# A block of attention: queries, keys and probabilities turned by VectorE blocks and a way through device memory

## The reference

```python
x = x + _L0_xattn_ref(_layernorm(x, axis=-1), ctx_4096, Wq, Wk, Wv, Wo, q_norm_w, k_norm_w)

def _L0_xattn_ref(latents, context, Wq, Wk, Wv, Wo, q_norm_w, k_norm_w):
    kv = jnp.concatenate([context, latents], axis=1)
    q = (latents @ Wq).reshape(bsz, q_len, HEADS, HEAD_DIM).transpose(0, 2, 1, 3)
    k = (kv @ Wk).reshape(bsz, kv_len, KV_HEADS, HEAD_DIM).transpose(0, 2, 1, 3)
    v = (kv @ Wv).reshape(bsz, kv_len, KV_HEADS, HEAD_DIM).transpose(0, 2, 1, 3)
    q = rms_norm(q, q_norm_w)
    k = rms_norm(k, k_norm_w)
    qg = q.reshape(bsz, KV_HEADS, groups, q_len, HEAD_DIM)
    scores = jnp.einsum('bhgqd,bhkd->bhgqk', qg, k) * scale
    probs = jax.nn.softmax(scores.astype(jnp.float32), axis=-1).astype(q.dtype)
    out = jnp.einsum('bhgqk,bhkd->bhgqd', probs, v)
    return out @ Wo
```

## Time and profile before

| | us |
|---|---|
| Median of 3 runs | 1143.39 (1141.55 to 1143.66) |
| Profiled execution | 1142.94 |
| Its span in the trace | 1141.1 |
| TensorE busy, matmuls | 1097.6 |
| VectorE / ScalarE / GpSimd busy | 773.4 / 523.9 / 398.5 |

### The profile page before, as it was taken

One profiled execution on the slowest core, in us unless ns is written; L12 is line 12 of the kernel. 1 busy time (PEld: TensorE's weight loads), 2 busy tenths in 40 slices (PEclk: granted clock), 3 DMA queues, 4 the chain that ended last, 5 costly groups with the idle time before them and its releaser, 6 DMA issues. The chain is left out here.

```text
span 1141.1 us, 18735 instructions
## 1 busy us (share of the span) xinstructions
PE 1097.6 (96%) x6533; PEld 950.9 (83%) x6533; DVE 773.4 (68%) x1496; ACT 523.9 (46%) x1398; POOL 398.5 (35%) x385
## 2 busy tenths in 40 slices
PE   4899999999999999999999999999999999888998
PEld 3789899998989999898989989878877777677877
DVE  7577777777777777777777765764344566889863
ACT  4354544545455454544544444443223445465531
POOL 4443343433334343343434321210002334575521
PEclk7899999999999999999999999999999999999999
DMA  6322323332332323233232120022202244143300
GB/s 221 82 79 71 104 63 98 88 96 69 92 103 64 97 89 96 68 102 106 70 103 84 50 91 1 1 80 89 65 1 56 65 111 111 43 104 77 84 10 37
DMA packets 65376, 89.05 MB, mean 78 GB/s; under 512 B 15544, under 2 KB 35024, under 8 KB 65284
## 3 DMA queue, kind: packets, MB, share of 16 engines
q1 hardware_dynamic: 60788, 70.95, 22.0%
q0 software_dynamic: 4496, 16.91, 4.8%
HBM read 64.64 MB, written 10.74 MB: 66 GB/s over the span
## 5 line engine op out<-in xcount | busy, mean ns | idle before, releaser
L366 PE MATMUL bank<-wqkv,kvT 128*128 128x256 f32 x1536 | 199.9, 286 | 2.1 <-DVE vv L570 2.1
L418 PE MATMUL bank<-wo,aoT 128*128 128x512 f32 x768 | 191.8, 398 | 0.0
L366 PEld LDWEIGHTS bank<-wqkv,kvT 128*128 128x128 f32 x1536 | 187.9, 191 | 3.7 <-DVE vv L570 3.6
L354 PE MATMUL bank<-wqkv,kvT 128*128 128x512 f32 x768 | 189.1, 395 | 1.6 <-DVE qn L585 1.6
L354 PEld LDWEIGHTS bank<-wqkv,kvT 128*128 128x128 f32 x768 | 141.8, 191 | 28.9 <-issue 1.8
L418 PEld LDWEIGHTS bank<-wo,aoT 128*128 128x128 f32 x768 | 139.6, 188 | 27.2
L671 POOL TENSOR_TENSOR rms<-msq,half_neg 128x4 f32<-128x4 f32 x64 | 80.0, 1249 | 202.7 <-DVE msq L581 202.5
L527 ACT ACTIVATE qsq<-bank 128x512 f32<-128x512 f32 x64 | 38.2, 597 | 115.3 <-PE bank L354 115.3
L553 ACT ACTIVATE prob<-bank,nmax 128x128 f32<-128x128 f32 x256 | 90.1, 371 | 2.2 <-DVE nmax L595 2.2
L585 DVE TENSOR_TENSOR qn<-bank,rms 128x512 f32<-128x512 f32 x64 | 44.3, 692 | 61.0 <-POOL rms L671 61.0
L674 POOL TENSOR_TENSOR rms<-msq,half_neg 128x2 f32<-128x2 f32 x64 | 44.8, 699 | 116.5 <-DVE msq L591 116.5
(11 more groups left out here) (176 smaller groups left out, 2131.1 us busy)
## 6 DMA issues: line engine op xcount, KB each, us to landing
wqkv_raw<-in_L_xattn_Wq_dram SPq DMA_DIRECT2D x32, 256.0 KB, 2.6
wo_raw<-in_L_xattn_Wo_dram SPq DMA_DIRECT2D x32, 256.0 KB, 2.8
qS<-qhl SPq DMA_DIRECT2D x32, 256.0 KB, 3.8
wload<-w_gu SPq DMA_DIRECT2D x20, 256.0 KB, 3.2
w_gu<-qch SPq DMA_DIRECT2D x16, 256.0 KB, 2.3
kS<-chl SPq DMA_DIRECT2D x32, 128.0 KB, 3.1
qch<-_L_ffn_down_qweight_dram SPq DMA_DIRECT2D x10, 256.0 KB, 3.6
w_d<-qch SPq DMA_DIRECT2D x10, 256.0 KB, 2.0
```

Source lines behind the costliest of these rows:

```text
L354: mm = pe.matmul(b_q[:, :], kvT[:, l, kt, p, 1:3, :], wqkv[:, par, r, kt, 0:QW], start=(kt == 0 and n == 0), stop=(kt == KT - 1 and n == 2))
L366: mm = pe.matmul(b_kv[:, b * 256:(b + 1) * 256], kvT[:, l, kt, p, 2 * b:2 * b + 2, :], wqkv[:, par, r, kt, QW:QKV], start=(kt == 0 and n = ...
L418: mm = pe.matmul(b_o[:, :], aoT[:, l, h, :, :], wo[:, par, r, h, :], start=(h == 0 and n == 0), stop=(h == G - 1 and n == 2))
```

## The change

The transposes by TensorE go. In place of them VectorE turns blocks of 32 x 32 numbers: it writes the normalized tile into a PSUM bank `b_n` in an order in which every fourth column stands together, and transposes blocks from there to SBUF (`qB`, `kB`, `pB`). SyncE stores the tile to device memory (`q_turn`, `k_turn`, `p_turn`, 256, 128 and 256 KB) and loads it back with whole blocks in their places (`blocks_out`, `blocks_back`). Queries arrive in `qT`; keys in `kT`, where ScalarE scales them in place; probabilities in the LO half of `pT`, from which ScalarE rounds HI, and VectorE subtracts in place at the head of its next step.

Squares are now summed by ScalarE's accumulator, in four and two instructions, so VectorE's two reductions go. Keys and values alternate between two banks. TensorE's scores move to the end of the step, its values product from unit j-2 to j-3 and to the place behind the query projection; exponentials and normalization move to unit j-2; the sum into `acc` (L566) moves from unit j-4 at the head to unit j-3 at the end of VectorE's list. The dequantization pieces stand behind the maxima and ahead of the key normalization. The first three weight tiles of the second part are loaded within the loop, in its steps 62 to 64.

```diff
+            def sp_step0(st):
+                if st.has(1, UNITS):
+                    sp.wait_ge(s_k_out, st.done(1, 16))
+                    wait(sp, s_s, st.done(2))
+                    blocks_back(sp, kT[:, :, :, :], k_turn).then_inc(s_k_back, 16)
+                if st.has(2, UNITS):
+                    sp.wait_ge(s_pB, st.done(2))
+                    wait(sp, s_p_back, st.done(3, 16))
+                    blocks_out(sp, p_turn, pB[:, :, :, :]).then_inc(s_p_out, 16)
+                if st.j >= 1:
+                    weight_load(st.j - 1)
+                sp_stores(sp, st.j)
...
+                for f in WLOAD_AT.get(st.j - EVEN_DONE, ()):
+                    weight_tile(sp, f)
+                if st.has(2, UNITS):
+                    sp.wait_ge(s_p_out, st.done(2, 16))
+                    wait(sp, s_pv, st.done(3))
+                    blocks_back(sp, pT[:, LO, :, :, :].bitcast(F32), p_turn).then_inc(s_p_back, 16)
+                if st.has(0, UNITS):
+                    sp.wait_ge(s_qB, st.done(0))
+                    wait(sp, s_q_back, st.done(1, 16))
+                    blocks_out(sp, q_turn, qB[:, :, :, :]).then_inc(s_q_out, 16)
+                sp_loads(sp, st.j)
+                if st.has(0, UNITS):
+                    sp.wait_ge(s_kB, st.done(0))
+                    wait(sp, s_k_back, st.done(1, 16))
+                    blocks_out(sp, k_turn, kB[:, :, :, :]).then_inc(s_k_out, 16)
+                    sp.wait_ge(s_q_out, st.done(0, 16))
+                    wait(sp, s_s, st.done(1))
+                    blocks_back(sp, qT[:, :, :, :], q_turn).then_inc(s_q_back, 16)
+        def blocks_out(sp, to, frm):
+            return sp.dma_start(to.rearrange("a p r -> (a p r)").rearrange("(p c) -> p c", p=P),
+                                frm.rearrange("p b h t -> p (b h t)"))
+        def blocks_back(sp, to, frm):
+            return sp.dma_start(to.rearrange("p a h t -> p a (h t)"), frm.rearrange("a p r -> p a r"))
...
         def dve_step0(st):
+            if st.has(3, UNITS):
+                dve.wait_ge(s_phi, st.done(3))
+                dve.tensor_tensor(pT[:, LO, :, :, :].rearrange("p h b t -> p (h b t)"),
+                                  pT[:, LO, :, :, :].rearrange("p h b t -> p (h b t)").bitcast(F32),
+                                  pT[:, HI, :, :, :].rearrange("p h b t -> p (h b t)").bitcast(F32),
+                                  ALU.subtract).then_inc(s_plo, 1)
...
+                dve.tensor_tensor(b_n[:, :].rearrange("p (b a k) -> p b a k", b=4, a=4),
+                                  prob[:, :, :].rearrange("p a (k b) -> p b a k", b=4),
+                                  rsum[:, :].unsqueeze(1).unsqueeze(3).to_broadcast([P, 4, 4, 32]),
+                                  ALU.mult).then_inc(s_pn, 1)
+                dve.wait_ge(s_pn, st.done(2))
+                wait(dve, s_p_out, st.done(3, 16))
+                dve.transpose(pB[:, :, :, :].rearrange("p b h t -> p (b h t)"), b_n[:, :]).then_inc(s_pB, 1)
...
         def act_step0(st):
+                for h in range(G):
+                    act.activation(b_sq[:, h * HD:(h + 1) * HD], b_q[:, h * HD:(h + 1) * HD], ACT.Square,
+                                   accum_out=ssq[:, h:h + 1]).then_inc(s_qsq, 1)
...
+                act.wait_ge(s_p_back, st.done(2, 16))
                 wait(act, s_pv, st.done(3))
+                act.activation(pT[:, HI, :, :, :], pT[:, LO, :, :, :].bitcast(F32), ACT.Copy).then_inc(s_phi, 1)
```

More of the change, by code:

```diff
@@ L369, in key_projection, with pe_scores0 @@
             mm.then_inc(s_kv, 1)
+        def pe_scores0(pe, st):
+            pe.wait_ge(s_q_back, st.done(1, 16))
+            pe.wait_ge(s_kT, st.done(1))
+            wait(pe, s_exp, st.done(2, 4))
+            for n in range(4):
+                mm = pe.matmul(b_s[:, n * P:(n + 1) * P], qT[:, n, :, :], kT[:, :, n // 2, :], start=True, stop=True)
+            mm.then_inc(s_s, 1)
         def pe_step0(st):
@@ L374, in pe_step0 @@
                 query_projection(pe, st)
-            if st.has(1, UNITS):
-                pe.wait_ge(s_qn, st.done(1))
-                wait(pe, s_qT, st.done(2))
-                wait(pe, s_kT, st.done(2))
-                for h in range(G):
-                    pe.transpose(b_tq[:, h * P:(h + 1) * P], qn[:, h, :], ident[:, :])
-                pe.wait_ge(s_kn, st.done(1))
+            if st.has(3, UNITS):
+                _, _, par = unit(st, 3)
+                pe.wait_ge(s_plo, st.done(3))
+                pe.wait_ge(s_vlo, st.done(3))
+                wait(pe, s_aolo, st.done(4))
@@ L397, in pe_step0 @@
[L397 to L399 removed]
+            if st.j == UNITS:
+                pe_scores0(pe, st)
+            if st.j == UNITS:
+                pe.wait_ge(s_qms, UNITS)
+                pe.wait_ge(s_kn, UNITS - 1)
+                pe.wait_ge(s_vlo, UNITS - 1)
                 x2_transposes(pe, 0)
                 x2_transposes(pe, 1)
[L402 to L407 removed]
@@ L423, in pe_step0 @@
                 x2_transposes(pe, 3)
[L424 to L433 removed]
+            elif st.has(1, UNITS):
+                pe_scores0(pe, st)
         def weight_piece(st):
@@ L833, in sp_ffn @@
             sp.wait_ge(s_kv, EVEN_DONE)
-            for f in range(FT):
+        def sp_ffn(sp):
+            for f in range(3, FT):
                 weight_tile(sp, f)
```

265 lines of the change are left out of this document (123 added, 142 removed).

## The result

The changed kernel takes 1210.46 us (median of 4 runs, 1208.58 to 1213.86) against 1142.71 us before (1141.55 to 1143.66): a ratio of 1.059, 95% interval 1.057 to 1.061. It is slower by 68 us, where 1120 us was forecast, and lies outside the range of 1088 to 1165. The profiled execution has a span of 1206.8 us, 65.7 us more than before.

A forecast was written before the change was run, and what follows sets the result against it. TensorE's matmuls bound the loop before; afterwards the probabilities' ring would, at 10.7 us in 53 steps and 10.25 in ten: 28 us saved, 5 lost at the end, 1142.94 - 28 + 5 = 1120 us, range 1088 to 1165.

The forecast's parts named there:

- TensorE's list: Matmuls of one attention step, the limit before at 11.08 us; ten transposes leave it, 0.92 us a step.
- the floor of 10.16: TensorE's remaining work per attention step, in us; as a rival (0.13) TensorE stays the limit and the kernel takes 1090 us.
- The ring: Probabilities' closed chain through VectorE, ScalarE and device memory, one turn per step: 10.22 us, 10.7 with delays under dequantization.
- The stepped read: VectorE's normalization reading every fourth word: taken at 0.69 us like a contiguous operation, bounds 0.69 and 1.38.
- the rival that costs half again: Stepped read in the normalization 0.35 us dearer, steps about 11.05 us, kernel 1142 us; chance 0.10.
- The doubled cost: Rival: stepped read costs double, +0.69 us in the ring's normalization, steps 11.4 us, kernel 1163 us; chance 0.20.
- The way back: Load of the turned probabilities from device memory, in 512 byte runs: 2.9 us, bounds 2.6 and 3.2.
- The queueing: SyncE's weight pieces and stores between the probabilities' way out and back: 0 to 0.65 us late, 0.3 on average.
- the dequantization: VectorE's dequantization piece between maxima and reciprocal: 0.4 us late in every second step, 0.2 on average.
- They do not decide: Said of other added waits, such as the keys' and queries' ways through memory, back well before wanted at 19.4 us.
- The tail: Last query projection to last output product: 33.1 us before, three ring turns and more give 38, so 5 us lost.
- late way back: Rival: probabilities return in 3.2 to 3.5 us under new traffic, +0.3 to 0.6 us a step, 1139 to 1158 us; chance 0.17.

The follow-up runs named there:

- e4: The changed kernel with VectorE's maxima ahead of the low part and ScalarE's weight rounding behind the exponentials: 1163.0 us.
- e1: The changed kernel with the block transpose of the probabilities done twice: 1249.6 us.
- e2: The changed kernel with the block transpose of the queries done twice: 1208.5 us.
- e3: The changed kernel with TensorE reading the keys in steps of four, so VectorE's normalization of the probabilities reads runs of 32 words: 1196.5 us.
- e5: The changed kernel with the probabilities turned by TensorE again; only queries and keys go through device memory: 1126.4 us.
- e9: e5 with the last four steps, behind the last projections, written out in another order: 1109.8 us.
- e8: The changed kernel with SyncE's row reordered: probabilities out, keys back, probabilities back, then weight pieces and stores of dequantized rows: 1263.7 us.
- e12: e8 with ScalarE's scaling of the returned keys moved behind the squares of the next keys: 1207.5 us.
- e15: The changed kernel without loads of quantized weights and gathers of table rows from the third chunk on: 1199.3 us.
- e16: e4 without loads of quantized weights and gathers of table rows from the third chunk on: 1125.8 us.

## Why the prediction was wrong

**TensorE's list: right.** Ten transposes less are worth 0.92 us a step; e4 reached 10.00 us, below the floor of 10.16. The clock stayed at 1.00 in the loop.

**The ring as the mechanism: right**, by e1 against e2. Six of its terms were met: low part, maxima to reciprocal 2.27 (2.27 forecast), reciprocal, block transpose 0.75 (0.77), way out 2.02 (2.0), copy and hand overs 0.66 (0.74).

**The stepped read: wrong step.** "I take 0.69": it measured 1.11 to 1.13, the rival that costs half again. The row on which the choice leaned, eight writes of 24 elements, says nothing of a read of 512 from SBUF. With the ring as the limit this was 0.41 us a step, an estimated 25 us (e3 and its turns; the time itself gave 14, as TensorE's read and SyncE's row took the rest). The queries' stepped read, from PSUM, was free. The doubled cost didn't occur.

**The way back: mis-sized.** 2.9 us forecast, 3.20 in quiet steps: +0.3. With the two terms a quiet turn is 10.22 + 0.41 + 0.30 - 0.08 (hand overs) = 10.85 us, as measured. Put into the sum one at a time they give 63 x 0.41 = 26 us, 1146, or 63 x 0.30 = 19 us, 1139: near the kernel before, not behind it by 68.

**The queueing, "0.3 on average": mis-sized.** The loaded steps are 1.04 us longer than the quiet ones, where 0.3 for the queue and 0.2 for the dequantization stood. Over all loaded turns the way back has 0.57 of the delay, the way out 0.37, the wait for a blocked SyncE 0.08, and the dequantization, forecast at 0.2, 0.07. The prediction priced what stands between the way out and back as bytes hidden by the wait for the way out, but the way back lands behind all of them: 3.20 us with none ahead, 3.46 with a weight piece, 3.99 with a piece and a store. It named what is queued behind SyncE's wait for the probabilities, and not that the probabilities are queued behind the waits for the keys and queries. "They do not decide", it said of these: they don't need the time themselves, but they hold the row. In the change that is the small term; in e4, where the ring is shorter, it is 0.49 us a turn.

**The tail: wrong step.** 5 us more forecast, 20 measured. It was priced as three turns of the ring. What it missed: without the projections nothing covers the order, in which low parts stand behind an addition, the x2 work and weight pieces (16 us from e5 to e9; in the change itself not run), and the clock falls behind the idle time (0.86 from 770 to 830 us; 1.00 from 726.85 to 760 us in the kernel before).

The sum of the misses: 54 loaded steps, 0.83 us longer than before where 0.38 shorter was forecast, 65; quiet steps 5 x 0.64 = 3; tail 15; up to Q(4) 2 lost, where the forecast had four steps 0.83 shorter, 5: together 88 of the 89 us between the forecast and the measured span. Two rivals, half again and late way back, happened together; each had been priced alone.

**Open.** Why the keys' store lands in 4.0 us with the loads and gathers and in 1.9 to 2.3 without was not taken apart: the loads go through SyncE's own queue, the gathers through GpSimd's, and both were left out together. Among the orders tried there is none in which none of the three ways is late.

## What to carry to other kernels

A round trip through device memory is cheap where its result is wanted a step later, and costs its full latency where it lies in a closed ring; count, for every chain that comes back to itself, all its terms, and double one of them to see (e1 against e2). Waits in an in-order row of DMA issues count for everything behind them: with six issues and their landing waits in one row, each of the orders tried here made one of the ways late. When a change moves work a step later, look at the last steps on their own, where the cover is gone: here that order was worth 16 us, half the profit of the better kernel (1109.8 us).

## What the runs showed of the hardware

- A VectorE operation that reads 512 elements 16 bytes apart: 1.11 us from SBUF, 0.70 from PSUM (contiguous 0.70). ScalarE's stepped PSUM read of 128: 366 ns, as without a step.
- TensorE's stepped read of the moving operand in fp32 takes the scores from 0.80 to 1.58 us for four products.
- The way back of 256 KB in 512 byte runs landed in 3.0 us ahead of other pieces in its queue (e8, e12), in 3.6 to 3.9 behind them (e4, e15, e16), whether 204 or 155 GB/s were moved beside it. A store of 128 KB landed in 4.0 us in the change (192 GB/s) and 3.8 in e5 (168), and without the loads and gathers in 2.3 (e15, 155) and 1.9 (e16, 173): the mean rate alone doesn't tell it.
- TensorE's granted clock stood at 1.00 in the loop and fell to 0.50 behind an idle time of 6.61 us in the change.
